# Three-set tails and early row stores in a four-layer graph network kernel

## The reference, cut to what matters

```python
h = features                                  # [12500, 128]
for _ in range(3):                            # one "typed pass" each
    t = einsum('nd,kod->kno', h, W_et) + b_et[:, None, :]      # 4 edge types
    a = segment_sum(t[etypes, src], dst, num_segments=N)
    gi = a @ W_ih.T + b_ih;  gh = h @ W_hh.T + b_hh            # 3 x 128 columns each
    r = sigmoid(ir + hr);  z = sigmoid(iz + hz)
    n = tanh(in_ + r * hn)
    h = (1 - z) * n + z * h
gate = sigmoid(concat([h, features]) @ i_w.T + i_b)
out = layernorm(features + gate * (h @ j_w.T + j_b))
```

## Time and profile before

| | |
|---|---|
| Median of three runs | 12868.93 us |
| Profiled execution, its own time | 12887.27 us |
| Span of its trace, first to last instruction | 12885.5 us |
| PE (TensorE matmul) busy | 9625.4 us, 75% |
| DVE (VectorE) busy | 4892.2 us, 38% |
| ACT (ScalarE) busy | 1747.4 us, 14% |
| POOL (GpSimd) busy | 8987.1 us, 70% |
| TensorE's mean granted clock | 0.809 of full speed |

### The profile page before, as it was taken

One profiled execution on the slowest core, in us unless ns is written; L12 is line 12 of the kernel. 1 busy time (PEld: TensorE's weight loads), 2 busy tenths in 40 slices (PEclk: granted clock), 3 DMA queues, 4 the chain that ended last, 5 costly groups with the idle time before them and its releaser, 6 DMA issues. The chain is left out here.

```text
span 12885.5 us, 166462 instructions
## 1 busy us (share of the span) xinstructions
PE 9625.4 (75%) x37162; PEld 5869.8 (46%) x37163; DVE 4892.2 (38%) x18947; ACT 1747.4 (14%) x4400; POOL 8987.1 (70%) x8364
## 2 busy tenths in 40 slices
PE   5777777788667777555555666599996999789995
PEld 3444444322465555443434444344443444445553
DVE  3333333555233333333334444333333333334443
ACT  1111111222220000000000111011110000012221
POOL 1888888877207777677776777577775777767774
PEclk7555555777788888677767777799998999899997
DMA  8999899899885555344434555388874888567773
GB/s 292 228 220 221 219 222 220 130 112 116 173 174 119 122 121 119 79 109 109 109 90 122 141 142 141 112 254 252 253 241 141 253 253 254 183 194 234 234 232 113
DMA packets 2877809, 2271.87 MB, mean 176 GB/s; under 512 B 1207747, under 2 KB 2650944, under 8 KB 2877478
## 3 DMA queue, kind: packets, MB, share of 16 engines
q1 hardware_dynamic: 2402284, 1630.55, 42.6%
q0 software_dynamic: 443536, 623.45, 25.0%
q10 hardware_dynamic: 31722, 15.04, 0.4%
HBM read 1536.88 MB, written 760.24 MB: 178 GB/s over the span
## 5 line engine op out<-in xcount | busy, mean ns | idle before, releaser
L1662 PE MATMUL bank<-work 128*128 128x512 f32 x4704 | 2136.3, 597 | 129.4 <-DMA work<-t_pairs 84.9
L1085 POOL DMA_INDIRECT ring<-t_types,stage x1692 | 1632.1, 965 | 762.3 <-issue 504.1
L1060 POOL DMA_INDIRECT t_sums<-ring,stage x1124 | 1744.3, 1552 | 447.8 <-issue 265.0
L2177 DVE TENSOR_TENSOR acc<-acc,bank 128x128 f32 x1686 | 483.3, 287 | 3913.1 <-PE bank L1682 3824.2
L1085 POOL DMA_INDIRECT ring<-t_x,stage x1128 | 1088.7, 965 | 933.5 <-ACT stage L1279 594.7
L1682 PE MATMUL bank<-ring 128*128 128x128 f32 x6768 | 1090.7, 312 | 688.9 <-DMA ring<-t_x,stage 321.0
L1682 PEld LDWEIGHTS bank<-ring 128*128 128x128 f32 x6768 | 980.2, 218 | 1069.9 <-issue 462.5
L1662 PEld LDWEIGHTS bank<-work 128*128 128x128 f32 x4704 | 853.3, 191 | 1002.0 <-issue 852.3
L1085 POOL DMA_INDIRECT more_rows<-t_types,stage x840 | 831.0, 989 | 256.0 <-issue 255.4
L2200 DVE TENSOR_SCALAR ring<-iota_f,meta_low 128x128 f32<-128x128 f32 x4496 | 1008.0, 301 | 0.0
L1537 PE MATMUL bank<-aux 128*128 128x128 f32 x2248 | 522.3, 407 | 555.6 <-ACT aux L1211 554.9
(11 more groups left out here) (330 smaller groups left out, 14560.3 us busy)
## 6 DMA issues: line engine op xcount, KB each, us to landing
work<-t_pairs SPq DMA_DIRECT2D x588, 1024.0 KB
t_pairs<-acc SPq DMA_DIRECT2D x560, 640.0 KB
work<-t_pairs SPq DMA_DIRECT2D x588, 256.0 KB
t_types<-work SPq DMA_DIRECT2D x216, 512.0 KB, 7.4
work<-t_types SPq DMA_DIRECT2D x294, 256.0 KB
aux<-t_pairs SPq DMA_DIRECT2D x196, 256.0 KB, 4.7
work<-t_x SPq DMA_DIRECT2D x108, 256.0 KB
ring<-t_types,stage POOLq DMA_INDIRECT x1692
```

Of the source, the lines that this page charges most:

```text
L1060: pool.indirect_dma_start(TAB[k], bass.IndirectOffsetOnAxis(ap=stage[:, u:u + 1], axis=0), msg[:, u, :], None, compute_op=ALU.add).then_in ...
L1085: pool.indirect_dma_start(gathered[par][u], None, table, bass.IndirectOffsetOnAxis(ap=stage[:, par * U + u:par * U + u + 1], axis=0)).then ...
L1662: mm = pe.matmul(o, dense_t[:, tile, k_ * D:(k_ + 1) * D], dense_b[:, half, :, k_ * HALF:(k_ + 1) * HALF], start=first and k_ == 0, stop=e ...
L2177: v.tensor_tensor(into, into, bank[q][:, 0:P], ALU.add).then_inc(added, 1)
```

## The change

The three tail steps of passes 4, 5 and 6 no longer follow one another in one set of buffers. There are three sets: the old one, one with banks 0 and 1 and pieces of `msg`, `hot` and `work`, and one with banks 2 and 3 and pieces of `more_rows`, `hot` and `work`. The second half of typed rows of each set goes through banks 4 and 5. Each engine has the three steps written out side by side in its stream. In pass 6, SP waits for the last dense block, loads the residual rows of the three tail steps at once, waits for the 33 steps between the gathers, stores all rows but the first 12 tiles (`out_most`, 6 DMAs), and stores those 12 tiles with one DMA when all steps are done. TensorE waits at the start of passes 5 and 6 until VectorE has read the banks, and in all six passes VectorE waits for its memset of `acc` (in pass 1 for that of `aux` too). If an input needs more than 36 steps, a branch does the rest one after another; this input doesn't take it.

```diff
+        home = StepSet(True, bank[6], bank[7], bank[6:8], g_r, g_z, g_a, g_y, g_c, g_rows, fin_x, 0)
+        tail_sets = [
+            home._replace(second=bank[4:6]),
+            StepSet(False, bank[0], bank[1], bank[4:6], in_msg[:, 0:GN], in_msg[:, GN:2 * GN], in_msg[:, 2 * GN:3 * GN],
+                    in_msg[:, 3 * GN:4 * GN], in_hot[:, 0:GN], [in_msg[:, 2 * GN:4 * GN], in_msg[:, 0:2 * GN]],
+                    work[:, 10 * GN:11 * GN], 1),
+            StepSet(False, bank[2], bank[3], bank[4:6], in_more[:, 0:GN], in_more[:, GN:2 * GN], work[:, 8 * GN:9 * GN],
+                    work[:, 9 * GN:10 * GN], in_hot[:, GN:2 * GN], [work[:, 8 * GN:10 * GN], in_more[:, 0:2 * GN]],
+                    work[:, 0:GN], 0)]
 # every engine
-        def tail_steps(eng, total, step):
-            for j in range(TAIL_STEPS):
-                step(STEPS + j)
+        def tail_steps(eng, total, step, together=None):
+            if together is not None:
+                together()
+            else:
+                for j in range(TAIL_STEPS):
+                    step(STEPS + j)
 # SP, passes 4 and 5
+                def types_together():
+                    store(STEPS - 1)
+                    for j in range(TAIL_STEPS):
+                        store(STEPS + j, tail_sets[j])
...
 # SP, pass 6
+                def rows_together():
+                    sp.wait_ge(dense_done, 6 * UNITS)
+                    for j in range(TAIL_STEPS):
+                        load(STEPS + j, tail_sets[j])
+                    sp.wait_ge(fin_rows, STEPS)
+                    out_most(rows_out[0])
...
+                    sp.wait_ge(fin_rows, total)
+                    out_rows(0, TAIL_STEPS * A, rows_out[0])
-            sp.wait_ge(fin_rows, total)
-            whole = (NG - 1) * A
...
 # ScalarE
+            def state_together(k):
+                gates(i0, at=s0)
+                gates(i1, at=s1)
+                new_state(i0, at=s0)
+                gates(i2, at=s2)
+                new_state(i1, at=s1)
+                new_state(i2, at=s2)
 # TensorE
+                if ph > 4:
+                    pe.wait_ge(types_rows, total * (2 * ph - 8))
+            def state_together(n):
+                gate_sums(i0, g0, (4 + n) * ADDS, at=s0)
+                gate_sums(i1, g1, (4 + n) * ADDS, at=s1)
+                state_sums(i0, g0, at=s0)
+                gate_sums(i2, g2, (4 + n) * ADDS, at=s2)
+                state_sums(i1, g1, at=s1)
+                state_sums(i2, g2, at=s2)
+            def tail_types(i, at):                      # after state_together, for each set in turn
+                pe.wait_ge(h_ready, i + 1)
+                type_sums(at, 0, (at.low, at.high))
+                wait(pe, types_rows, i * 2)
+                type_sums(at, 1, at.second)
+            def fin_together():
+                for j, i in enumerate(state_together(2)):
+                    fin_turn(i, STEPS + j, tail_sets[j])
+                for j in range(TAIL_STEPS):
+                    fin_sums(STEPS + j, tail_sets[j])
+                for j in range(TAIL_STEPS):
+                    fin_turn_back(STEPS + j, None, tail_sets[j])
 # VectorE
+                            v.wait_ge(feat_added, PAD + 1)
+                        v.wait_ge(added, (ph - 1) * ADDS + (PAD + 1))
+            def state_together(n):
+                state_sums_(i0, n, s0)
+                state_mix_(i0, g0, s0)
+                state_sums_(i1, n, s1)
+                state_sums_(i2, n, s2)
+                state_mix_(i1, g1, s1)
+                state_mix_(i2, g2, s2)
+            def types_together(n):
+                for i, at in zip(state_together(n)[0], tail_sets):
+                    type_rows(i, 0, at, (at.low, at.high))
+                    type_rows(i, 1, at, at.second)
+            def fin_together():
+                nodes_ = state_together(2)[1]
+                for j in range(TAIL_STEPS):
+                    fin_product(STEPS + j, tail_sets[j])
+                fin_moments(STEPS, None, tail_sets[0])
+                fin_moments(STEPS + 1, None, tail_sets[1])
+                fin_norm(STEPS, nodes_[0], tail_sets[0])
+                fin_moments(STEPS + 2, None, tail_sets[2])
+                fin_norm(STEPS + 1, nodes_[1], tail_sets[1])
+                fin_norm(STEPS + 2, nodes_[2], tail_sets[2])
```

More of the change, by code:

```diff
@@ L1 @@
+from collections import namedtuple
 from contextlib import ExitStack
@@ L83 @@
 ZA = -(-PAIR_LEN // (ZEROS * P * 64)) * 64
+StepSet = namedtuple("StepSet", "home low high second r z a y c rows x slot")
 LAST_OUTS = -(-(N - (NG - 1) * GN) // P)
 DEPTH = 4
+MOST = (ST - LAST_OUTS - TAIL_STEPS * A) // DEPTH
 LOOPS = NG // DEPTH
@@ L762, in features_in, with stream_pass @@
                         unit(q - 1)
-            def stream_pass(ph, table, load, store, late=None):
+            def stream_pass(ph, table, load, store, late=None, together=None):
                 def body(p, units):
@@ L808, in step @@
                         late(m - 1)
+                if together is not None:
+                    together()
+                    return
                 tail_steps(sp, total, step)
@@ L862, in state_pass, with out_rows @@
-                if n < 2:
+                def types_together():
+                    store(STEPS - 1)
+                    for j in range(TAIL_STEPS):
+                        store(STEPS + j, tail_sets[j])
+                    with sp.If(total - (STEPS + TAIL_STEPS) > 0):
+                        with turns(sp, STEPS + TAIL_STEPS, STEPS + NG) as m:
+                            store(m)
                     for hh in range(2):
                         sp.wait_ge(types_out[hh], total * (16 * (n + 1)))
+                def out_rows(first, last_, done):
+                    sp.dma_start(out[first * P:last_ * P, :].rearrange("(a p) f -> p a f", p=P),
+                                 by_tile(acc[:, first * D:last_ * D], last_ - first)).then_inc(done, 16)
@@ L865, in _ @@
+                stream_pass(4 + n, TT[n % 2], load, store, None, types_together if n < 2 else rows_together)
             for n in range(3):
                 state_pass(n)
-            sp.wait_ge(fin_rows, total)
-            whole = (NG - 1) * A
[L871 to L878, removed]
         @block.gpsimd
@@ L1721, in step @@
                         late[q](m, g)
[L1722 removed]
+                tail_steps(pe, total, step, together)
             now = [0]
@@ L1814, in part @@
                         pe.wait_ge(h_ready, i + 1)
[L1815 to L1818, removed]
+                    type_sums(home, hh, bank[6:8])
                 return part
-            def fin_turn(i, g, done, normed_):
+            def tail_types(i, at):
@@ L1827, in fin_turn, with fin_sums @@
                 mm.then_inc(fin_turned, 1)
[L1829 to L1836, removed]
+            def fin_sums(m, at=home):
+                pe.wait_ge(fin_copied, m + 1)
+                pe.matmul(at.low[:, :], wT[:, W_I, :], at.c, start=True, stop=False)
+                pe.matmul(at.low[:, :], wT[:, W_I + 1, :], at.r, start=False, stop=True)
+                pe.matmul(at.high[:, :], wT[:, W_J, :], at.c, start=True, stop=True).then_inc(fin_prod, 1)
@@ L2446, in fin_link_, with type_rows @@
-            def fin_link_(ins, m, n):
-                ins.then_inc(fin_link, 1)
-                v.wait_ge(fin_link, m * 3 + n)
-            def fin_product(i, g, normed_):
-                v.wait_ge(fin_prod, now[0] + 1)
-                v.wait_ge(fin_gate, now[0] + 1)
-                v.scalar_tensor_tensor(out=g_y, in0=bank[7][:, :], scalar=jb_col[:, 0:1], in1=g_z, op0=ALU.add,
+                    state_sums_(i, n)
+                    state_mix_(i, g)
+                return part
+            def type_rows(i, hh, at, banks):
+                v.wait_ge(h_ready, i + 1)
+                v.wait_ge(types_prod, i * 2 + (hh + 1))
+                for a in range(2):
+                    ins = v.tensor_tensor(at.rows[hh][:, a * KT * D:(a + 1) * KT * D], banks[a][:, :], bet_all[:, :], ALU.add)
+                ins.then_inc(types_rows, 1)
```

210 lines of the change are left out of this document (132 added, 78 removed).

## The result

The changed kernel takes 12691.61 us (four runs, 12686.07 to 12698.69) against 12871.55 us before (now the median of four runs), a ratio of 0.9862 with a 95% interval of 0.9846 to 0.9878. That is 180 us less; I had forecast 106.5 less and a range from 12744 to 12800. The direction was right, but the gain was 1.7 times what I had forecast.

What follows compares the result with a forecast made beforehand. GpSimd's gathers were taken to set the pace, with serial gaps between passes and a final store. Savings of 30.3 + 27.6 + 31.2 + 19.4, less 2, made 106.5 us, hence 12763 us, range 12744 to 12800.

Steps and rivals of the forecast that it cites:

- (a): VectorE's six waits for its memset at the pass starts: taken as 0, at worst 9 us lost.
- So it is the memset ... that lets the gathers go: Start of the next pass: the `acc` memset, 11.15 us long, holds the first gather, which takes 10.02 us, until it ends.
- Tails of passes 4 and 5: Three tail steps side by side: 36.7 us in place of 67.0 and 37.5 in place of 65.1.
- late T matmuls: Typed-row matmuls of a half of rows in the tails: 2.1 us each at full clock, 3.5 at half clock.
- Tail of pass 6: The last three steps side by side: 51.8 us for 83.05, 31.2 off, between 47 and 56.
- term (c): Registers for three steps read at once at the head of a tail: 2 us added in all.
- The store: Most of the result stored before the final tail: 24.4 us behind the last step become 5.0, 19.4 off.
- Rival 4: More gain than counted, from a store or start that shrinks too: 12740 us; chance 0.04.
- Rival 2: The early store goes out only when pass 6's tail is over: gain 19 less, 12782 us; chance 0.05.
- Rival 3: Gathers of passes 4 to 6 lose their pace: 0.032 us more each eats the whole gain; chance 0.05.
- rival 1: TensorE stays at half clock through the tails: some 15 us more in each, 12808 us; chance 0.10.
- Terms (b) to (e): TensorE's wait in passes 5 and 6: 0; register reads: 2 us; gathers beside `out_most`: likely 0; wait before residual loads: 0.

Runs made afterwards that it cites:

- e1: The kernel before with only VectorE's waits for its memsets added, against the kernel before: 12808.73 us, ratio 0.9942.
- e2: The changed kernel with VectorE's waits for its memsets taken out: 12752.79 us, ratio 0.9898 to the kernel before.
- after_asserts: The changed kernel with run-time assertions of the bounds of a few loaded numbers and nothing else: 12693 us, ratio 0.9857 to the kernel before.
- e7: The changed kernel with a second memset of `acc` ahead of the other, each with a wait behind it: ratio 0.9857 to the kernel before.
- e8: The kernel before with a 128x128 fp32 copy directly behind the memsets and no wait: ratio 0.9988 to the kernel before.
- e5: The kernel before with the early store of the result alone: 12851.3 against 12871.3 us, ratio 0.9985.
- e9_rows_ahead_of_mix: The changed kernel with set 0's typed rows added ahead of set 2's state mix in passes 4 and 5: ratios 0.9874 and 0.9894 to the kernel before.

## Why the prediction was wrong

- **The failed step is (a), "Six waits for the memset on VectorE ... I take 0"**, with bounds of 0 and a loss of 9. The wait is worth 71 us alone (e1) and 59 in the change (e2 against `after_asserts`), and the six long gathers that it does away with were 64 us. It is most of what I missed, 73.5 us. Of these 64 us 37 lie in passes 1 to 3, for which my sum has no other term at all.
- It failed because of the reading ahead of it: **"So it is the memset ... that lets the gathers go"**. The row was right (10.02 us for a gather that ends 0.9 us behind the memset), the cause wrong, and so was the sign that I named for it: in the changed kernel the first gather of pass 5 takes 0.94 us. e7 has two memsets and no held gather; e8 has a held gather with a copy in line. I took overlap for cause, and the one instruction that starts the moment the memset ends stood in the earlier trace rows itself, at 9842.65.
- The Trainium skill, in "SBUF — State Buffer", section "Who interferes with whom", names copies, casts and `tensor_scalar` as what can take the shared port pair, and says that a VectorE instruction with at most one SBUF input, outside the two-port modes, doesn't contend. By that a memset can't hold a gather. I applied the page's rule to it all the same; e7 agrees with the page, with gathers of 0.94 us beside two memsets. The page has "whoever issues first" get the pair. Read with that rule, e8 says that a copy which hasn't begun, and waits for the engine, has the pair already. What the runs themselves show is the held gather (10.03 us), not the pair.
- The trace of before also held the contrary case. In pass 1 the memset of `acc` has another memset behind it, and that of `aux` has the one-hot block. The gathers in the kernel before, pass 1:

```profile
3842.05 11.15 DVE L2215 MEMSET acc<- 128x13312 f32 x1 [2.72 <-issue]
...
3847.16 0.94 POOL L1085 DMA_INDIRECT more_rows<-t_x,stage  x1 [0.30 <-issue]
...
3852.17 0.95 POOL L1085 DMA_INDIRECT more_rows<-t_x,stage  x1 [0.30 <-issue]
3853.42 13.48 POOL L1085 DMA_INDIRECT more_rows<-t_x,stage  x1 [0.30 <-issue]
...
3855.70 10.30 DVE L2218 MEMSET aux<- 33x12288 f32 x1 [2.50 <-issue]
...
3865.93 2.33 DVE L2200 TENSOR_SCALAR ring<-iota_f,meta_low 128x128 f32<-128x128 f32 x12
```

  Gathers run at their pace through the first memset and are held through the second. I had read pass 4 to 5 alone, and had not looked for the same memset elsewhere. The held gather starts 2.3 us ahead of the second memset's row, in VectorE's pause. That pause seems to be part of the memset: 2.72 + 11.15 us for 13312 columns and 2.50 + 10.30 for 12288 are both 1.04 ns a column. That is an estimate from these two rows.
- **Tails of passes 4 and 5** (30.3 and 27.6 forecast): 31.4 and 30.4 by the trace, from 67.0 to 35.6 and 65.1 to 34.7. Right to 2.8 us. I had taken the late T matmuls at full clock. In pass 5 they were: the last twelve take 5.42 us at a granted clock of 1.00. In pass 4 they take 7.11 us, for the clock is 0.50 from 9735.7 to 9739.0. TensorE had been idle for 3.06 us ahead of these twelve in both passes, so that pause alone doesn't explain the fall.
- **Tail of pass 6** (31.2): 35.4, inside its bounds. The three `fin_sums` took 9.3 us, not 11.5. The three tails together gave 97 us where my sum, less the 2 of term (c), has 87. That is 10 more of the 73.5.
- **The store** (19.4): 19.4 by the trace (24.4 to 5.0), 20 in e5. Right, and the gathers beside it kept their pace.
- "The gathers of the next pass therefore shift with VectorE's last addition, one to one": nearly so in the outcome, but not by the memset. The gathers now wait for the landing of the stores, and that moves with the last addition: the first gather is at 9747.90, 4.7 us behind it.
- **Rivals**: none named the wait. Rival 4, "a store or start that shrinks too", put 0.04 on 12740 without a mechanism. Rival 2 fell, since the early store is issued at 12575.62. Rival 3 fell too: passes 4 and 5 are 41.7 and 40.2 us shorter, and their tails and long gathers alone give 41.8 and 39.5, so the gathers kept their pace. So did rival 1: the granted clock was 0.89 and 0.92 in the tails of passes 4 and 5, and 0.82 in the first 20 us of the last tail. In the row below, of the changed kernel, TensorE is busy for 18.25 of these 20 us.

```profile
12640.00:12660.00 20.00, 18.25 (x36) 7.95 (x37) 5.52 (x8) 4.51 (x7) 0.00 (x0) 0.82 0.00 0
```

The terms as the traces and runs have them: tails 97, store 19 to 20, waits 59 to 71. Together 175 to 188, for 180 measured. Terms (b) to (e) of the prediction, 2 us in all, have no run of their own; this sum leaves little room for more.

## What to carry to other kernels

- When an instruction of GpSimd is many times its usual length, look at what VectorE starts right after it ends, not only at what VectorE runs meanwhile. In this kernel a long memset with a 128x128 copy or `tensor_scalar` next in line holds a gather until the memset is over. A wait on the memset's semaphore, or an instruction of 128x2 between, frees it, and costs half a microsecond or less of VectorE.
- A wait that looks like pure cost deserves a look at what it keeps out of a queue. Price it by what stands behind it on its engine, and by what the other engines do meanwhile.
- For a serial tail that the engine which sets the pace waits out, laying the instructions out by hand from single durations was right to 3 us in 36 and to 4 in 48. The rows stored before the tail cost nothing here, where the DMA had room (0.31 of it busy just behind the store).

## What was not expected of the hardware

- With a 128x128 fp32 copy of 0.17 us queued behind an 11.15 us memset, a gather took 10.03 us; with a 128x2 one-hot or a 128x2 copy in the same place none was held.
- In each of two groups of runs the kernel before took 14788 and 14679 us, 14 to 15% more than elsewhere, with single gathers as long as ever (median 0.945 to 0.947 us) and a mean TensorE clock of 0.76 to 0.77 for 0.81. Within pass 4 of `e9_rows_ahead_of_mix` (9300 to 10900 us) GpSimd waited 211 us in 64 places ahead of gathers into `ring` for a `stage` of ScalarE, in pauses of up to 6.5 us. In pass 4 of `after_asserts` (8300 to 9700 us) there was no such pause over 0.3. DMA moved 199 GB/s there for 237 in `after_asserts`. That may mean that rows land later on those chips; neither this nor its cause was tried.
